# Two scan layers: batch 0's second block merged and gated by GpSimd, batch 0 projected in the last state

## The reference

```python
xb, z = split(rmsnorm(x) @ in_w.T)          # 256 channels each
xb = silu(conv(xb) + cb)
delta, B, C = parts of xb @ xp_w.T          # delta = softplus(delta @ dt_w.T + dt_b)
for t in range(1024):                       # for each batch, channel e, state n
    v = 0.6 * v + delta[t] * B[t, n] * xb[t]
    h = exp(delta[t] * -exp(a_log)) * h + v
    y[t] = sum over n of h * C[t, n]
x = x + ((y + dp * xb) * silu(z)) @ out_w.T
```

## Time and profile before

| | |
|---|---|
| median of 3 runs | 1168.22 us (1168.12 to 1169.85) |
| profiled execution, its own time | 1178.23 us |
| span of the profiled execution | 1176.9 us |
| PE busy | 1046.0 us (89% of the span) |
| DVE busy | 981.1 us (83%) |
| ACT busy | 816.3 us (69%) |
| POOL busy | 503.1 us (43%) |
| mean granted clock of PE | 0.934 |

### The profile page before, as it was taken

One profiled execution on the slowest core, in us unless ns is written; L12 is line 12 of the kernel. 1 busy time (PEld: TensorE's weight loads), 2 busy tenths in 40 slices (PEclk: granted clock), 3 DMA queues, 4 the chain that ended last, 5 costly groups with the idle time before them and its releaser, 6 DMA issues. The chain is left out here.

```text
span 1176.9 us, 21254 instructions
## 1 busy us (share of the span) xinstructions
PE 1046.0 (89%) x7779; PEld 656.3 (56%) x7779; DVE 981.1 (83%) x1312; ACT 816.3 (69%) x1621; POOL 503.1 (43%) x482
## 2 busy tenths in 40 slices
PE   6899999999999879889998989889998994699992
PEld 4222222222223244478987865478887873488982
DVE  6999999999994677879998966989998986867754
ACT  4289898999998537978986715898886712355551
POOL 5401340101011130048987851059896732445653
PEclk9689999999999898899999999899998995799997
DMA  5110000000000500139998940138998949111114
GB/s 160 61 42 16 29 16 28 16 29 16 16 2 17 146 19 3 57 72 227 247 239 178 243 103 3 57 84 203 241 248 186 235 94 286 13 35 42 42 39 119
DMA packets 58519, 114.94 MB, mean 98 GB/s; under 512 B 15422, under 2 KB 28734, under 8 KB 58416
## 3 DMA queue, kind: packets, MB, share of 16 engines
q0 software_dynamic: 15024, 50.76, 21.4%
q1 hardware_dynamic: 40152, 60.62, 17.1%
q10 hardware_dynamic: 3240, 2.20, 0.7%
HBM read 55.47 MB, written 9.13 MB: 55 GB/s over the span
## 5 line engine op out<-in xcount | busy, mean ns | idle before, releaser
L2220 PEld LDWEIGHTS m_pair<-filter_w,delta_x_t 128*128 128x128 f32 x2560 | 299.2, 195 | 53.4 <-issue 53.3
L2220 PE MATMUL m_pair<-filter_w,delta_x_t 128*128 128x112 f32 (+3 forms) x2560 | 303.4, 278 | 20.9 <-DVE x_inner L2238 10.6
L555 DVE TENSOR_REDUCE neg_max<-max_ps 128x1 f32<-128x1024 f32 x256 | 295.7, 1215 | 15.0 <-PE max_ps L544 14.8
L671 ACT ACTIVATE exp_scores<-score_k 128x512 f32<-128x512 f32 x512 | 270.8, 607 | 28.5 <-PE score_k L663 22.7
L2196 ACT ACTIVATE decay<-delta,a_log 128x1024 f32<-128x1024 f32 x128 | 145.8, 1142 | 66.6 <-DVE normed L2247 32.1
L544 PE MATMUL max_ps<-k_rows,q_rows 48*128 48x512 bf16 x512 | 163.0, 400 | 12.4 <-DVE neg_max L555 10.8
L2188 ACT ACTIVATE filter_w<-filter,b_t 128x112 f32<-128x112 f32 (+1 forms) x576 | 167.3, 374 | 0.0
L663 PE MATMUL score_k<-q_rows,k_rows 51*128 51x512 bf16 x512 | 162.9, 389 | 2.4 <-ACT exp_scores L671 0.6
L690 PE MATMUL av_ps<-exp_scores,v_cols 128*32 128x256 f32 x2048 | 158.1, 393 | 0.0
L564 POOL CAST neg_max_parts<-neg_max 128x16 bf16<-128x16 f32 x16 | 3.1, 196 | 235.1 <-DVE neg_max L555 235.1
L2238 DVE TENSOR_TENSOR_SCAN m_pair<-decay,m_pair 128x1024 f32<-128x1024 f32 x40 | 91.5, 2287 | 6.7 <-PE m_pair L2220 6.4
(11 more groups left out here) (336 smaller groups left out, 1628.3 us busy)
## 6 DMA issues: line engine op xcount, KB each, us to landing
c_row<-c_rows SPq DMA_DIRECT2D x64, 512.0 KB, 5.6
x_inner<-normed POOLq DMA_DIRECT2D x16, 512.0 KB, 6.4
x_inner<-h_t POOLq DMA_DIRECT2D x15, 512.0 KB, 6.4
delta_x<-mod_memory POOLq DMA_DIRECT2D x14, 512.0 KB, 7.9
delta_x<-x_inner POOLq DMA_DIRECT2D x14, 512.0 KB, 8.0
mod_memory<-h_t POOLq DMA_DIRECT2D x14, 512.0 KB, 9.8
mod_memory<-normed POOLq DMA_DIRECT2D x12, 512.0 KB, 9.9
gate_up_all<-in_gate_up_w SPq DMA_DIRECT2D x8, 512.0 KB, 7.1
```

The source lines that it names most:

```text
L555: ve.tensor_reduce(nm[leg % 2][:, 4 * j + qt:4 * j + qt + 1], mps[:, bank:bank + 2, :].rearrange("p a q -> p (a q)"), AX_X, ALU.max, negat ...
L671: ac.activation(pt[a % 4][:, HEADS[r % 4], :], eps[:, bank, :], ACT.Exp, scale=SC).then_inc(*exped.up())
L2220: mm = pe.matmul(vps[blk][:, lo:hi], self.duT[b][:, c, blk * P:(blk + 1) * P], wf[g % 3][:, lo:hi], start=True, stop=True)
```

## The change

The kinds of states change in batch 1 (states 3 and 5 of it from B to D, state 13 from A to B). `sum_slots` places the sums of a joined place four and five states behind it instead of five and six, others one state behind. POOL issues a join ahead of the second block's product. Batch 0's merge is a product instruction of POOL instead of a transfer, and POOL gates block 1 of batch 0 in state 5; DVE gates block 0 in state 4. In the last state PE projects batch 0 into the PSUM pair that the first scan has left, ahead of the remaining sums. The last state's block 1 is multiplied, added and gated by DVE in both layers, around the adds of batch 0 that the new `Tail` hands on. In `mamba_inputs` and `mamba` batch 1's projection is issued from there; on PE it stands ahead of the turn of batch 0, on DVE the adds of batch 1 come behind the turns. The diff, cut to its core:

```diff
 CPL_COLS = ("cn_b1", "cn_b2", "cn_b3", "cn_w4", "cn_b4", "gc_b1", "gc_b2", "gc_w3", "gc_b3", "adaptive_range")
-KINDS = ("AD" + "AB" * 7 + "AB" * 6 + "AAAA") + ("AD" * 3 + "AB" * 5 + "AB" * 6 + "AAAA")
+KINDS = ("AD" + "AB" * 7 + "AB" + "AD" * 2 + "AB" * 4 + "AA") + ("AD" * 3 + "AB" * 5 + "AB" + "AD" * 2 + "AB" * 4 + "AA")
+Tail = namedtuple("Tail", "out product add gate_first gate_second")
 def sum_slots(first):
...
     end = first + n - 1
-    slots, closing = {g: [] for g in range(first, end + 2)}, []
+    slots, closing = {g: [] for g in range(first, end + 1)}, []
     places = [g for g in range(first, end + 1) if KINDS[g] == "A"]
...
         for c in range(2):
-            at = min(g + (5 if joined else 2) + c, again if again == end else again - 1)
-            slots[end + 1 if g == end else at].append((g, c))
+            at = min(g + 4 + c if joined else g + 1, again - 1, end)
+            slots[at].append((g, c))
         if i + 1 == len(places) or (places[i + 1] - first) // DS > batch:
...
         halves = self.halves
-        self.ring.bind(halves[:4])
-        y_ready = None
+        tail = None
         for l in range(NL):
-            y_ready = self.mamba_scan(l, in_w_all, y_ready)
+            self.ring.bind(halves[:4])
+            tail = self.mamba_scan(l, in_w_all, tail)
+        ve.wait_ge(*self.inputs_gated)
+        added = [self.ve_out(self.X, c, tail.out[c]) for c in (0, 1)]
+        tail.product()
+        roots = [self.ln_root(self.X, 0, TB, added)]
+        tail.add()
+        gated = tail.gate_second()
+        for t in range(TB):
+            self.ve_center(t, 1, 3)
+        gated += tail.gate_first()
+        self.ring.bind(halves[6:], first=6)
+        out = self.pe_out(NL - 1, 1, gated, self.s_hs.at())
         self.ring.bind(halves[4:], first=4)
-        gated = [y_ready[0](), y_ready[1]()]
-        for engine in (pe, ve):
-            engine.wait_ge(*self.inputs_gated)
-        out = self.pe_out(NL - 1, 0, gated[0], (self.s_hs.sem, self.s_hs.n - 1))
-        out.update(self.pe_out(NL - 1, 1, gated[1], self.s_hs.at()))
-        added = [self.ve_out(self.X, c, out[c]) for c in (0, 1)]
-        roots = [self.ln_root(self.X, 0, TB, added)]
         added += [self.ve_out(self.X, c, out[c]) for c in (2, 3)]
         roots.append(self.ln_root(self.X, TB, NT, added[2:]))
-        for t in range(TB):
-            self.ve_center(t, 1, 3)
         shifted = [self.ve_shift(self.N, t, 1, 3, roots[0]) for t in range(TB)]
...
                 pe.wait_ge(*mids[blk, b - 1])
+            for m in wide_free:
+                pe.wait_ge(*m)
             for c in range(2):
...
         else:
-            out = self.pe_out(l - 1, 0, y_ready[0](), self.s_hs.at())
-            ready = {c: [self.ve_out(self.xm, c, out[c])] for c in (0, 1)}
+            ready = {c: [self.ve_out(self.xm, c, tail.out[c])] for c in (0, 1)}
+            tail.product()
             root = self.rms_stats(self.xm, ready, 0)
-            last_gate = y_ready[1]()
+            tail.add()
+            gated = tail.gate_second()
+            gated += tail.gate_first()
             for c in (0, 1):
                 self.ve_rms_norm(c, root)
-            out = self.pe_out(l - 1, 1, last_gate, self.s_hs.at())
-            ready = {c: [self.ve_out(self.xm, c, out[c])] for c in (2, 3)}
+            ring.bind(self.halves[6:], first=6)
+            out = self.pe_out(l - 1, 1, gated, self.s_hs.at())
+            ring.bind(self.halves[:4])
             turn(0)
             turn(1)
+            ready = {c: [self.ve_out(self.xm, c, out[c])] for c in (2, 3)}
+            wide_free.extend(ready[2] + ready[3])
             pe_l(0)
...
             ac_conv_first(0, bank["f", 0])
+            ve_taps(1, bank["l", 1])
             pe_f(1)
             pe_x(0)
-            ve_taps(1, bank["l", 1])
             ac_conv_last(1)
...
         pe.wait_ge(*read)
-        pe.wait_ge(*gated)
+        for m in gated:
+            pe.wait_ge(*m)
         for c in (2 * b, 2 * b + 1):
...
             return KINDS[:g + 1].count("A") - 1
+        def by_second(g):
+            return g + 1 - (g + 1) // NS
         def join(g):
...
                 wait_from(sp, yg0.sem, by_pool(g - 3))
-                wait_from(sp, yg.sem, g - 2)
+                wait_from(sp, yg.sem, by_second(g - 3))
+                if (g - 2) % NS == 0:
+                    sp.wait_ge(*self.last_product)
             sp.dma_start(csb[g % 3][:], self.c_dram[l, b, n:n + 1, :].to_broadcast([P, S])).then_inc(
...
         def pe_skip(b):
-            wait_from(pe, gated.sem, NBLK * (NB * l + b - 1) + 1)
+            wait_from(pe, gated.sem, NB * l + b)
             pe.wait_ge(*self.diag_set.at())
...
             po.wait_ge(hs.sem, NBLK * g + 2)
-            if n == 1:
-                wait_from(po, gated.sem, NBLK * (NB * (l - 1) + b + 1))
             po.tensor_tensor(yacc[b][1] if n == 1 else hh[g % 4], hh[g % 4], csb[g % 3][:], ALU.mult).then_inc(*yg.up())
...
                 return
-            po.wait_ge(yg.sem, g + 1)
+            po.wait_ge(yg.sem, by_second(g))
             wait_from(po, *acc_in[n % 2].at())
...
                 po.wait_ge(*acc_in[k].at())
-            po.dma_start(yacc[b][0], yacc[b][1], accum_op=ALU.add).then_inc(*merged.up(16))
-            ended[b] = merged.at()
+            po.tensor_tensor(yacc[b][0], yacc[b][0], yacc[b][1], ALU.add).then_inc(*added.up())
+        def po_gate_second(b):
+            po.wait_ge(*added.at())
+            po.tensor_tensor(zs[:, 1, b, :], zs[:, 1, b, :], yacc[b][0], ALU.mult).then_inc(*added.up())
+            return added.at()
         def po_add_last(b, n):
             g = state(b, n)
-            po.wait_ge(yg.sem, g + 1)
+            po.wait_ge(yg.sem, by_second(g))
             po.wait_ge(*acc_in[n % 2].at())
...
         def pe_sums(g):
-            if g in (G0, G0 + DS + 5):
+            if g in (G0, G0 + DS + 4):
                 pe_skip((g - G0) // DS)
...
                 pe_sum_half(at, c, (at, c) in closing)
-        def ve_last(b, n):
+        def ve_last_product(b, n):
             g, step = state(b, n), self.s_last
...
             ve.tensor_tensor(h, h, csb[g % 3][:], ALU.mult).then_inc(*step.up())
-            ve.wait_ge(*acc_in[1].at())
+            self.last_product = step.at()
+        def ve_last_add(b, n):
+            h, step = hh[state(b, n) % 4], self.s_last
+            ve.wait_ge(*ended[b])
             ve.wait_ge(*step.at())
-            ve.tensor_tensor(yacc[b][1], yacc[b][1], h, ALU.add).then_inc(*step.up())
-            ve.wait_ge(*acc_in[0].at())
-            ve.wait_ge(*added.at())
+            ve.tensor_tensor(h, h, yacc[b][0], ALU.add).then_inc(*step.up())
+        def ve_gate_first(b):
+            ve.wait_ge(*ysum.at())
+            ve.tensor_tensor(zs[:, 0, b, :], zs[:, 0, b, :], yps[:], ALU.mult).then_inc(*gated.up())
+            return gated.at()
+        def ve_gate_last(b, n):
+            step = self.s_last
             ve.wait_ge(*step.at())
-            ve.tensor_tensor(yacc[b][0], yacc[b][0], yacc[b][1], ALU.add).then_inc(*step.up())
-            ended[b] = step.at()
-        def ve_gate(b, blk):
-            ve.wait_ge(*(ysum.at(), ended.get(b))[blk])
-            y = (yps[:], yacc[b][0])[blk]
-            ve.tensor_tensor(zs[:, blk, b, :], zs[:, blk, b, :], y, ALU.mult).then_inc(*gated.up())
-            return gated.at()
+            ve.tensor_tensor(zs[:, 1, b, :], zs[:, 1, b, :], hh[state(b, n) % 4], ALU.mult).then_inc(*step.up())
+            return step.at()
         first_read, second_read, place_read, joined, ended = self.first_read, self.second_read, self.place_read, {}, {}
...
         first_done = None
-        self.mamba_inputs(l, in_w, y_ready, ac_filter, ac_decay, pe_momentum, po_skip)
+        self.mamba_inputs(l, in_w, tail, ac_filter, ac_decay, pe_momentum, po_skip)
         for g in range(3):
...
             if i + 1 == NS:
-                pe_sums(g)
+                self.ring.bind(self.halves[4:6], first=4)
+                if l == NL - 1:
+                    pe.wait_ge(*self.inputs_gated)
+                out = self.pe_out(l, 0, first_gated, (hs.sem, NBLK * g + 1))
             ve_scan_first(b, n)
-            if b and n == 5:
-                ve_gate(b - 1, 0)
+            if b and n == 4:
+                first_gated = [ve_gate_first(b - 1)]
             if kind(g) == "B":
...
             ve_scan_second(b, n)
-            if b and n == 6:
-                first_done = ve_gate(b - 1, 1)
-            if i and kind(g - 1) == "A" and (i < NS - 1 or l < NL - 1):
+            if i and kind(g - 1) == "A" and i + 1 < NS:
                 po_accumulate(*states[i - 1])
-            if i < NS - 1 or l < NL - 1:
+            if kind(g) != "A":
+                po_join(b, n)
+            if i + 1 < NS:
                 po_output_second(b, n)
             if kind(g) != "A":
-                po_join(b, n)
                 po_accumulate(b, n)
...
                 po_merge(b - 1)
```

(37 more changed lines are left out.)

2 lines of the change are left out of this document (1 added, 1 removed).

## The result

The changed kernel took 1160.5 us (median of 20 runs, 1152.69 to 1171.52), the kernel before 1168.94 in the same session (20 runs, 1164.65 to 1182.71). The ratio is 0.9909, 95% interval 0.9884 to 0.9934: faster, by some 10.6 us. The ratio leaves out the runs that fell into a slower state of the chip; the medians of all runs differ by 8.4 us. The prediction said 1152 within 1143 to 1163: its direction and range held, and it was 8.5 us too low, outside the 1143 to 1158 that it gave its own case.

A forecast was written before the change was run, and what follows sets the result against it. It took PE's chain, 5.32 us a state, as the bound, with time lost behind DVE's long gate and in the tails. 11.0 + 1.6 + 5.6 - 2.0 = 16.2 us won, so 1152 us, range 1143 to 1163.

The forecast's parts named there:

- its own case: The forecast without the rivals: 1152 us, own range 1143 to 1158, chance 0.60.
- the 11 states: Batch 1, first scan of state 1 to that of state 12: 5.5 us won in each layer, 11.0 together.
- rival 1: Transfers bind batch 1, shown by DVE or PE waiting on them in states 8 to 12: 1159.5 us, chance 0.20.
- The tails: Behind each layer's last state: layer 0's turn at F+16.6, 5.6 us won; layer 1's shift at F+23.65, 2.0 lost.
- F: The end of the last first-block scan in a layer, from which the times of the tails are counted.
- States 12 to 15: End of batch 1: 17.1 us before, 16.0 at 5.32 a state; 0.8 won in each layer, 1.6 for both.
- I place its release: Batch 0's merge on POOL: released some 6 us after the issue of state 3's accumulate, state 4's product 5 us late.
- the second scan's four buffers: Cover for POOL's lateness: a second scan needs the buffer of four states earlier, leaving about 6 us of slack, barely enough.
- The floor of 61.3: Least time for batch 1's 11 states, with DVE needing some 1 us more than PE over states 3 to 6.
- The join's place: Join ahead of the second product, with sums one state earlier: costs nothing while POOL is on time.
- Rival 3: PE falls to its lower clock in the D states, 5.6 us more a state: about 1185 us, chance 0.07.
- The start of the argument: Batch 1: DVE's gate took 5.35 us beside POOL's back-to-back products, POOL stood 9.13 us at the merge, PE idled 5.46.

The follow-up runs named there:

- run 8: The changed kernel again, unaltered: 1165.89 us, ratio 0.9927 to the kernel before.
- run 2: The changed kernel with DVE gating block 0 of batch 1 ahead of the eight centers in layer 1's tail: 1156.05 us.
- run 9: The kernel of run 7 with the row sums of layer 1's tail issued behind both gates: 1146.67 us, ratio 0.9792 to the kernel before.
- run 1: The changed kernel with POOL's merge of batch 0 waiting only for batch 0's own accumulates: 1150.94 us.
- after: The profile of the changed kernel itself, without further edits; its profiled span is 1159.2 us, its median time 1160.5 us.
- run 6: The changed kernel with the edits of run 1 and run 2 together: 1158.41 us, ratio 0.9865 to the kernel before.
- run 7: The kernel of run 6 with POOL's join behind the second block's product again: 1147.3 us, ratio 0.978 to the kernel before.
- Run 5: The kernel before with one edit, its merging transfer waiting only for batch 0's own accumulates: 1156.12 us, ratio 0.9857.
- run 3: The changed kernel with DVE, not POOL, gating block 1 of batch 0 behind state 6's second scan: 1165.56 us.

## Why the prediction was right, and where it was off

The changes did what the steps said, in order and mostly in size. The stretches won 13.0 us (11.6 in run 8) of the 16.2; the greatest part of that error is one term, the 11 states. The rest of the 8.5 us lies in the whole times, which gained less than the stretches; why stays open. That 1160.5 lies in the range is partly luck: the range reached up to 1163 for rival 1's sake, whose cause is wrong (below).

*The tails* came as worked out. Layer 0: turn at F+16.3 against F+16.6. Inside it two errors cancel: the last product, priced free of POOL, took 3.04 us (the row at 694.78), and PE's gap of 2.65 us, though longer than the 1.8 expected, left the projection at 3.81. Layer 1: F+23.42 against 23.65, again with two errors, 6.29 us of projection for 5.44 and no loss at the last product (1.22), for which 0.8 had been added. That they cancel is luck: both vary from profile to profile (5.18 and 1.72 us in run 8, F+22.70). The centers ahead of the gate were rightly named as a cause (run 2); the row sums ahead of it, which were not named, hold the projection up by 1.9 us more (run 9).

*States 12 to 15* gave half of the 0.8. The floor taken was 5.32 a state, but 14 and 15 are both of kind A, and two A states follow each other at 5.72 (682.13, 687.85), the pitch that the earlier trace rows had shown; the last late C row (0.41 us, 0.38 in layer 1) accounts for the rest. Free of lateness they take 16.40 (run 1).

*The 11 states* are the failed step: "I place its release some 6 us after that accumulate's issue (landings 4.5 to 11.9, median 8.0, this one with less beside it, since the join is now issued earlier), state 4's product 5 us late." The merge started 8.8 us after it; the median of its own row, 8.0, would have come near that. State 4's product then starts at 636.87, 9.5 us after its scan began, where run 1 has it right behind the scan: 7.1 us late (625.14 there, 601.90 and 606.50 being the starts of the stretches). The cover was taken from the wrong resource: it counted the second scan's four buffers, which by its own sum give some 6 us, but C rows have three places and take 6.1 us to come, and DVE's product ran out of these first. And the lateness, once there, falls by only 0.6 us in two states. What was lost to it, 1.2 and 2.2 in the prediction, is 3.9 and 2.8 in the first profile (64.61 and 63.54 against 60.69), 4.0 and 6.2 in run 8, the last with the clock's share. The floor of 61.3 was 0.6 too high. That layer 1 won just the 5.5 that was forecast is therefore luck: both errors cancel there, and in run 8 it won 2.2.

*The join's place* was costed at nothing "while POOL is on time". In layer 1 it cost 0.9 us in after and 1.35 in run 6 (run 7).

*Rival 1* is the instructive one: its sign appeared (DVE waits for C rows), its time, 1159.5, is nearer than the forecast's, and its cause is wrong. Transfers stood idle more than before, and did as much at a share of 0.98 once POOL was on time. A wait on a transfer tells that it landed late; whether the transfers were slow or it was issued late is read from the issue. (No row shows its 237 GB/s; the earlier trace rows give 228 to 235 at a full share, 2.2 to 2.3 us, so its sum stands.) *Rival 3's* fall of the clock came neither where nor for the reason given: not in the D states, but behind a late C row, in some runs.

*The start of the argument* was right as a row and wrong as a cause. The prediction read 5.35 us of gate beside POOL's back-to-back products, and 9.13 us of POOL at the merge, and let the change cure the first. Run 5 cures the second alone and gets more than the change does. The Trainium skill ("SBUF — State Buffer", Who interferes with whom) has the rule under which the gate stretches, DVE with two SBUF operands against GpSimd; the rows of run 5 show when the gate is spared: where POOL leaves a gap in which it can begin first. What it says of an operand in PSUM also agrees: the products at 650.95 and 662.84 kept their 1.23 and 1.22 us beside a POOL without a gap.

## What to carry to other kernels

Look at what a wait counts before moving work away from behind it: a semaphore shared by two batches makes a wait for the old one wait for the new one's transfers, and here one narrower wait alone won more between the first scan and the shift (15.6 us) than the whole rearrangement (13.0 and 11.6). Follow an engine's lateness to every buffer that it frees and take the one with the fewest places and the longest refill; an instruction that got long beside a busy neighbour is often the trace of that neighbour's lateness. Where the profile has a median for the very thing, use it.

## What the runs showed of the hardware that was not expected

- The length of a gap did not tell whether PE's clock falls. Behind 2.65 us (layer 0's tail in after) 32 matmuls ran at the upper level, 3.81 us; behind 2.09 (run 2) and 2.68 (run 8) 40 matmuls took 7.89 and 7.95 instead of 4.61, with the clock at 0.57 on the mean. What else decides was not tried.
- A product of DVE on two SBUF operands took 1.19 to 1.23 us where no large product of POOL had begun before it, and 1.72 (run 8) to 5.35 us where one had, or began with it within 0.02 us (4.14, run 3). Where DVE's began 0.2 to 0.3 us earlier, POOL's took 3.1 to 3.2 us instead of 2.35 (runs 5, 8 and 9). The 5.35 us spans two products of POOL without a gap, so such a gate can wait for more than one.
- POOL's rows of 2.6 to 3.0 us need care: in a row without gaps the products start some 2.3 us apart (644.63, 646.96 and 649.26 in after), so the rows overlap their neighbours and the products are no slower.
